# Two layer-0 chunks multiplied in fp32 without a split, and the maximum with zero taken as a reduction over pairs

## The reference

```
for W in filters:                       # layer 0: (1024, 128), layer 1: (4096, 128)
    z = einsum('bhd,bmd->bhmd', x0, prev).reshape(b, h*m, d)
    cur = relu(einsum('bpd,pn->bnd', z, W[0]))
    prev = cur; outs.append(cur)
result = concatenate(outs, axis=1).sum(axis=-1)      # (512, 256)
h = relu(concatenate([result, dense_ctx], 1) @ W_top1 + b_top1)
h = relu(h @ W_top2 + b_top2)
y = h @ W_top3
```

## Time and profile before

| | us |
|---|---|
| median of 3 runs | 1007.87 |
| their range | 1007.66 to 1015.26 |
| profiled execution, its own time | 1014.19 |
| span of the profile | 1012.1 |
| busy in the span: DVE, PE, POOL, ACT | 945.3, 909.8, 830.4, 814.2 |

### The profile page before, as it was taken

How to read it: one execution, slowest core, us unless ns; L and a number is a source line. 1 busy time by engine, 2 the same in 40 slices (tenths; PEclk the granted TensorE clock), 3 DMA queues, 4 the chain that set the end, 5 groups by cost and what they waited for, 6 DMA issues and landing times.

```text
span 1012.1 us, 17939 instructions
## 1 busy us (share of the span) xinstructions
PE 909.8 (90%) x3822; PEld 698.4 (69%) x3822; DVE 945.3 (93%) x902; ACT 814.2 (80%) x2808; POOL 830.4 (82%) x606
## 2 busy tenths in 40 slices
PE   3879999989989998998999899899989978999988
PEld 2567777667767766766776677687667866778754
DVE  4599999999999999999999999999999999999993
ACT  2777888888788887878888887888888867888872
POOL 5797899898889989888998988888898877987540
PEclk9999999999999999999999999999999988999997
DMA  6421222211222221122222112222211222112000
GB/s 185 124 80 56 68 69 70 69 40 39 71 67 67 69 69 36 42 71 67 68 69 69 41 38 71 67 67 70 60 33 55 71 64 69 26 54 63 1 1 0
DMA packets 42849, 61.18 MB, mean 60 GB/s; under 512 B 6273, under 2 KB 17153, under 8 KB 42786
## 3 DMA queue, kind: packets, MB, share of 16 engines
q1 hardware_dynamic: 38690, 58.48, 19.0%
q0 software_dynamic: 4096, 2.11, 1.4%
HBM read 56.37 MB, written 4.20 MB: 60 GB/s over the span
## 4 chain that ended last, share of the span: by engine, by line
PE 27%; issue 23%; DVE 19%; POOL 19%; ACT 7%; DVEq 1%; POOLq 1%; ACTq 0%
DVE c L545 10%; POOL z L316 8%; PE ps_y L640 7%; PE ps_y L646 6%; PE ps_y L641 6%; ACT prod L401 6%; POOL z_lo L309 5%; DVE csum L538 5%; DVE prod L524 4%; POOL prod L325 3%; POOL gat L290 3%; PE ps_c L627 1%; PE ps_c L628 1%; PE ps_c L629 1%; ACT z_hi L370 1%
## 5 line engine op out<-in xcount | busy, mean ns | idle before, releaser
L401 ACT ACTIVATE prod<-ps_y,es 128x128 f32<-128x128 f32 x2560 | 711.1, 432 | 153.9 <-PE ps_y L646 147.8
L640 PE MATMUL ps_y<-w_hi,c_hi 128*128 128x512 f32 x1024 | 423.6, 414 | 51.1 <-DVE prod L524 47.9
L538 DVE TENSOR_REDUCE csum<-prod 128x64 f32<-128x1536 f32 x256 | 446.7, 1745 | 10.9 <-ACT prod L401 0.6
L646 PE MATMUL ps_y<-w_hi,c_lo 128*128 128x512 f32 x1024 | 406.5, 397 | 1.5
L641 PE MATMUL ps_y<-w_lo,c_hi 128*128 128x512 f32 x1024 | 403.9, 394 | 0.0
L325 POOL TENSOR_TENSOR prod<-prod 128x1024 f32<-128x1024 f32 x128 | 308.4, 2409 | 81.3 <-DVE prod L524 47.1
L640 PEld LDWEIGHTS ps_y<-w_hi,c_hi 128*128 128x128 f32 x1024 | 194.7, 190 | 119.6 <-DVE prod L524 65.3
L524 DVE TENSOR_TENSOR prod<-ps_y,es 128x512 f32<-128x512 f32 x384 | 253.1, 678 | 23.5 <-PE ps_y L646 21.4
L646 PEld LDWEIGHTS ps_y<-w_hi,c_lo 128*128 128x128 f32 x1024 | 194.3, 190 | 55.0 <-DVE c_lo L505 12.1
L545 DVE TENSOR_SCALAR c<-csum 128x128 f32<-128x128 f32 x128 | 221.7, 1732 | 0.1
L641 PEld LDWEIGHTS ps_y<-w_lo,c_hi 128*128 128x128 f32 x1024 | 195.1, 191 | 34.2
(11 more groups left out here) (63 smaller groups left out, 266.3 us busy)
## 6 DMA issues: line engine op xcount, KB each, us to landing
second<-et_scratch SPq DMA_DIRECT2D x160, 256.0 KB, 4.4
first<-et_scratch SPq DMA_DIRECT2D x32, 256.0 KB, 3.2
et_scratch<-gat SPq DMA_DIRECT2D x64, 64.0 KB
prod<-w SPq DMA_DIRECT2D x4, 512.0 KB, 7.8
gat<-table,rows_now POOLq DMA_INDIRECT x128, 2.4
wt_sb<-wt SPq DMA_DIRECT2D x2, 512.0 KB, 6.3
prod<-w0a SPq DMA_DIRECT2D x1, 320.0 KB, 2.9
prod<-w0b SPq DMA_DIRECT2D x1, 320.0 KB, 3.2
```

The source lines that it names most:

```text
L401: last = nc.scalar.activation(prod[:, buffer_of(g, u), h // 2, :, h % 2], ps_y[:, bank_of(g, u, k), j * N:(j + 1) * N], ACT.Copy, scale=es ...
L538: nc.vector.tensor_reduce(csum[:, maps], prod[:, buffer_of(g, u), FOLD // 2:F // 2, maps, :].rearrange("p a n t -> p n a t"), AX.XY, ALU.a ...
L640: nc.tensor.matmul(out, hi, w_hi, start=True, stop=False)
L646: nc.tensor.matmul(out, lo, w_hi, start=False, stop=True).then_inc(y_ready, 1)
```

## The change

Chunks 0 and 1 of layer 0 are no longer split: PE multiplies the fp32 `z` with the fp32 weights `w0_sum` in one `matmul` call each, as soon as `z` is there. Their rounding on ACT and splitting on POOL (and in the first group on DVE and POOL) disappear; chunks 2, 3 and 4 are treated as before. The tables of the order are rewritten for that. `csum` gets a second column that is zero throughout (one `memset` at the start), and `rectify` becomes a `tensor_reduce` with max over the pairs (sum, 0). In the first group DVE does all five products and then the three splits that are left.

```diff
+WHOLE = 2
+SPLIT = KP - WHOLE
-        csum = sb("csum", [P, N])
+        csum = sb("csum", [P, N, 2])
...
             def multiply(g, k):
-                wait(pool, z_lo_ready, g.times(KP, k + 1 - KP))
+                if k < WHOLE:
+                    wait(pool, l0_done, g.times(1))
+                else:
+                    wait(pool, z_lo_ready, g.times(SPLIT, k + 1 - KP))
...
-            Z_AT = {0: ((1, 2), (1, 3)), 1: ((1, 4),), 3: ((2, 0), (2, 1))}
-            Z_LO_AT = {0: (0, 1), 1: (2, 3), 2: (4,)}
+            Z_AT = {0: ((1, 1), (1, 2), (1, 3)), 1: ((1, 4),), 3: ((2, 0),)}
+            Z_LO_AT = {1: (2, 3), 2: (4,)}
...
-            Z_HI_AT = {(2, 0): (3, 4), (2, 1): (3, 7), (1, 2): (0, 2), (1, 3): (0, 5), (1, 4): (1, 5)}
+            Z_HI_AT = {(1, 2): (0, 4), (1, 3): (0, 6), (1, 4): (1, 5)}
...
-                nc.vector.tensor_scalar(c1[:, u % 2, :], csum[:, :], 0.0, None, ALU.max).then_inc(c1_ready, 1)
+                nc.vector.tensor_reduce(c1[:, u % 2, :], csum[:, :, :], AX.X, ALU.max).then_inc(c1_ready, 1)
...
             def layer0(g, k):
                 if k == 0:
                     wait(pe, c_ready, g.times(1))
+                if k < WHOLE:
+                    pe.wait_ge(z_ready, g.times(KP, k + 1))
+                    nc.tensor.matmul(ps_c[:, :], w0_sum[:, k, :], z[:, k, :].rearrange("p (b u d) -> p u b d", u=TG, b=BT),
+                                     start=(k == 0), stop=False)
+                    return
...
-            Z_USED_AT = ((1, 1), (1, 4), (2, 1), (2, 4), (2, 6))
+            Z_USED_AT = ((0, 6), (1, 2), (1, 6), (2, 2), (2, 6))
```

More of the change, by code:

```diff
@@ L175, in tower @@
         ones_zeroed = sem("ones_zeroed")
+        csum_zeroed = sem("csum_zeroed")
         rows_staged = sem("rows_staged")
@@ L305, in split_z @@
             def split_z(g, k):
-                pool.wait_ge(z_hi_ready, g.times(KP, k + 1))
+                pool.wait_ge(z_hi_ready, g.times(SPLIT, k + 1 - WHOLE))
                 wait(pool, l0_done, g.times(1))
@@ L329, in _ @@
                 gather(Group(0, g), range(TG))
[L330 to L339, removed]
-            Z_AT = {0: ((1, 2), (1, 3)), 1: ((1, 4),), 3: ((2, 0), (2, 1))}
-            Z_LO_AT = {0: (0, 1), 1: (2, 3), 2: (4,)}
+            Z_AT_FIRST = {0: ((1, 0), (1, 1), (1, 2)), 1: ((1, 3), (1, 4)), 3: ((2, 0),)}
+            Z_LO_AT_FIRST = {1: (2,), 2: (3, 4)}
+            Z_AT = {0: ((1, 1), (1, 2), (1, 3)), 1: ((1, 4),), 3: ((2, 0),)}
+            Z_LO_AT = {1: (2, 3), 2: (4,)}
             def body(g, number):
@@ L409, in _ @@
                                      ACT.Copy).then_inc(w1_hi_ready, 1)
-            for k in range(KP):
+            for k in range(WHOLE, KP):
                 if k == LASTK:
@@ L465, in _ @@
             nc.vector.tensor_scalar(rows[:, :], neg[:, :], bounds_sb[:, 2:3], None, ALU.add).then_inc(rows_step, 1)
+            nc.vector.memset(csum[:, :, :], 0.0).then_inc(csum_zeroed, 1)
+            dve.wait_ge(csum_zeroed, 1)
             nc.vector.memset(ones_b[:, :], 0.0).then_inc(ones_zeroed, 1)
@@ L491, in multiply @@
                 dve.wait_ge(pairs_in[k], g.times(32, 32) if k == 0 else g.times(16, 16))
-                wait(dve, z_lo_ready, g.times(KP, k + 1 - KP))
                 nc.vector.tensor_tensor(z[:, k, :], first[:, :], second[:, k, :], ALU.mult).then_inc(z_ready, 1)
@@ L537, in reduce @@
                 maps = slice(half * N // HALVES, (half + 1) * N // HALVES)
-                nc.vector.tensor_reduce(csum[:, maps], prod[:, buffer_of(g, u), FOLD // 2:F // 2, maps, :].rearrange("p a n t -> p n a t"),
+                nc.vector.tensor_reduce(csum[:, maps, 0], prod[:, buffer_of(g, u), FOLD // 2:F // 2, maps, :].rearrange("p a n t -> p n a t"),
                                         AX.XY, ALU.add).then_inc(reduced, 1)
@@ L553, in _ @@
             turn(Group(0, 0))
[L554 to L557, removed]
+            for k in range(KP):
+                multiply(Group(0, 0), k)
+            for k in range(WHOLE, KP):
+                dve.wait_ge(z_hi_ready, k + 1 - WHOLE)
                 nc.vector.tensor_tensor(z_lo[:, k, :], z[:, k, :], z_hi[:, k, :].bitcast(F32),
                                         ALU.subtract).then_inc(z_lo_ready, 1)
-                for chunk in range(k + 2, min(k + 4, KP)):
-                    multiply(Group(0, 0), chunk)
             split_c(Group(0, 0), slice(0, 1), first_c, first_c_lo)
@@ L564, in _ @@
             sum_h0(Group(0, 0))
[L565 removed]
+            dve.wait_ge(z_lo_ready, SPLIT)
             dve.wait_ge(w_ready, 3)
@@ L612, in _, with layer0 @@
         def _(pe):
-            def layer0(g, k, number=None):
+            def layer0(g, k):
                 if k == 0:
                     wait(pe, c_ready, g.times(1))
[L617 to L622, removed]
+                if k < WHOLE:
[3 more added lines that the diff above has]
+                    return
+                pe.wait_ge(z_lo_ready, g.times(SPLIT, k + 1 - WHOLE))
                 high, low = (x[:, k, :].rearrange("p (b u d) -> p u b d", u=TG, b=BT) for x in (z_hi, z_lo))
```

7 lines of the change are left out of this document (3 added, 4 removed).

## The result

| | before | after |
|---|---|---|
| median, us | 1011.57 (1007.66 to 1016.76) | 902.35 (900.03 to 904.71) |
| ratio, 95% interval | | 0.892 (0.886 to 0.898) |
| profiled execution, span | 1014.19, 1012.1 | 904.71, 902.9 |
| start up to the first `c_hi` | 57.1 | 53.7 |
| 30 groups, to the last `c_hi` | 896.0 | 788.6 |

The lower three lines of the table cut the span at the same two instructions as the prediction: the loop gives 107.4 us, the start 3.4, and the end takes 1.6 back.

A forecast was written before the change was run, and what follows sets the result against it. VectorE, waiting for GpSimd, was taken as the bound, moving to TensorE at 26.5 us. Start 55.2, 30 groups at 26.9 with passages 819, end 57.5, and 2.1 around the span gave 934, rounded to 935 us; range 918 to 966.

The forecast's parts named there:

- the reduction over pairs: VectorE's `rectify`: 0.41 us instead of 1.732 on average, without waiting for GpSimd; VectorE's need falls from 28.5 to about 23.4 us.
- the fp32 call: TensorE, two whole layer-0 chunks a group: 1.05 us each against 0.71 for split ones, +0.7 us per group, between 0 and 0.7.
- handing over: Loop period: 0.4 us a group for imperfect passing of work between engines, added to TensorE's 26.5 us to give 26.9.
- passage: Loop branch from one iteration to the next: 1.5 us each, taken between 1.0 and 1.9, eight of them, 12 us.
- The check by `sum_h1`: Cross-check of the fp32 price: 0.23 us for a four-column call plus four passes at 0.213 us gives 1.07 us.
- irregular losses: Loop before the change: 14.7 us beyond regular periods and passages, likely from `rectify` of up to 9.6 us, expected to go.
- The end: Span after the last `c_hi`: 59.0 us to become 57.5, by losing four `rectify` waits, -1.5 us, between 0 and -4.
- low end of 918: Bottom of the forecast range in us, from TensorE's floor of 917: 26.55 us a group, 1.0 a passage, 4 saved at the end.
- (a): Rival: engines block each other in the loop; handing over costs 1.4 us a group, period 27.9, time 965 us; 20%.
- (b): Rival: the new `rectify` reduction waits for GpSimd after all; periods of 27.9 to 28.6 us, time 980 to 1000; 5%.
- (c): Rival: TensorE reaches chunk 2 before its split is there, so the kernel is slower; 1030 us at a 3.6 us wait; 3%.
- (d): Rival: fp32 calls amid fp32r ones cost more than 1.05 us; at 2.0 us the period is 28.8, time 990; 2%.

## Why the prediction was wrong, step by step

**Right.** That the `rectify` waits for GpSimd, that the reduction over pairs doesn't and costs 0.41 us, and that the bound moves to TensorE. VectorE has 23.7 us of work a group (said 23.4), ScalarE 24.0 (23.7), GpSimd 25.2 (25.2). GpSimd's 27.7 before was measured as 27.6 where it is the bound. The start took 53.7 us against 55.2. No gap shows ahead of chunk 2.

**Wrong in size.** The mechanism came as forecast; what failed are terms of the sum, and most of the miss lies in the loop: the fp32 call at 1.05 us, the 0.4 us a group for handing over, and the 1.5 us for each passage. The span came out at 902.9 against 931.7: 30.4 us less in the loop, 1.5 less at the start, 3.1 more at the end.

The fp32 call was taken at 1.05 us from the earlier trace rows and costs 0.86: two a group, 30 groups, 11.4 us. The rows were read rightly but come from calls whose weights change between 128 and 16 rows, which lays the load bare. The check by `sum_h1` didn't help: its 0.23 us is for the most part the load of a call with four columns (a load lasts 0.19 us), and with 512 columns that load is hidden behind the matmuls, so 0.23 + 4 x 0.213 adds what costs nothing there. Four passes at 0.213, half of the 0.43 between two records, give 0.85, the measured value. The Trainium skill's four passes (FP8 and Floating Point Precision, TensorE Precision Notes) were thus the better guide, at the pitch of these rows; the 0.95 worked out from them in the prediction was too high as well.

The 0.4 us for handing over, 12 us in all, was carried from an engine that waits in the middle of its work to one that doesn't. TensorE is busy for the whole window. Against this stands an addition that came out too low: by rows the need was 26.5 - 0.38 = 26.1, measured are 26.29, 5 us in 30 groups. If the other terms hold, a bank takes 0.687 us and not 0.68; that is an estimate, 26.29 less those terms over 32 banks. 11.4 + 12 - 5 is the 18.4 of the period.

The passages were carried over at 1.5 us each, 12 us, though nothing in the earlier trace rows says that they would survive the wait. The reduction alone, on the kernel before with its fetches, leaves at most 0.1 us of a passage, so they hung on the wait of the `rectify`. That is 18.4 + 12 = 30.4 us. The irregular losses were rightly taken to go; the prediction put them down to the long `rectify` alone, and the clock behind them was part of it. It said that the clock in the loop is full, which holds for its one window and not for the whole trace.

The end was expected to gain 1.5 us and lost 1.6. Up to the eight dense calls it gained 2.2 (29.4 us against 31.5), and behind them 0.1; the calls themselves took 3.8 more, 14.0 against 10.2, because six of them ran at 1.2 GHz where two had. In the other profiled execution the end took 52.7: this term is a matter of luck from one execution to the next.

The range's low end of 918 had kept the full fp32 price and 1.0 us for a passage, though the text named 0.71 as the other bound of the call. In hindsight, with the bounds that it had itself (0.7 us less for the calls, no handing over, no passages) it would have reached 30 x 25.8 + 55 + 55 + 2 = 886.

**The rivals.** (a) did not come: three engines at 90, 91 and 96% of the period don't disturb the fourth. (b) is refuted by the line of L544, (c) by the windows, (d) by the two measurements of the call.

## What to carry to other kernels

When the bound moves to another engine, work the new period out from that engine's own work, and let losses of the old bound (handing over, passages, irregular ones) go to zero at the range's low end: they belong to the engine that waited. A price read from rows holds for their neighbourhood; before it is used elsewhere, look at what stands between the calls, here the weight loads. A VectorE instruction whose maximum lies far over its minimum at one size can be a wait that the profile counts as work; look for a form of it that doesn't wait before making either engine's work smaller. And look at the granted clock of the whole span, not of one window: a wait can cost once more behind its end.

## What the runs showed of the hardware

- A `tensor_scalar` of 128 numbers a partition lasts up to 9.6 us beside an unbroken run of GpSimd (6.3 with the layer 0 of the kernel after), a `tensor_tensor` of two operands in SBUF up to 6.4, a `tensor_reduce` of 256 numbers at most 0.42.
- An fp32 matmul of 512 columns takes 0.86 us at 2.4 GHz, 1.05 when the weights change between 128 and 16 rows, and 2.0 at 1.2 GHz with that change.
- The clock falls in the dense part in some executions of the same kernel and not in others. The two profiled ones differ by 8 us, nearly the spread of the kernel's ten.
- Between the first and the last `c_hi` it fell only in the four traces whose `rectify` waits, in stretches of 3.4 and 6.8 us at 1.2 GHz.
- Instruction fetches at a loop's branch (a ScalarE body of 371 or 378 instructions, none at 362) cost at most 0.1 us where ScalarE has slack.
